# Stacked attentions of a four-layer transformer: masked keys placed by transfers through DRAM into tiles of kept zeros, and routing steps in other slots

## What is computed

```python
x = x + xattn0(layernorm(x), ctx); x = x + ffn0(layernorm(x))      # prototypes, low rank
x = x + xattn1(layernorm(x), ctx); x = x + ffn1(layernorm(x))      # shared and routed experts
x = x + xattn2(layernorm(x), ctx, mask); x = x + ffn2(layernorm(x))  # 8 experts, top 2, capacity
x = x + xattn3(layernorm(x), ctx)                                  # causal mask
h = layernorm(x, scale, shift); x = x + self_attention(h)          # causal, 128 keys
x = x + moe(layernorm(x, scale, shift))
# in ffn2: position of a token at its expert = running count over all tokens; beyond cap it is dropped
# every attention: softmax(q k^T / sqrt(8)) v, then Wo
```

## Time and profile before

| quantity | value |
|---|---|
| runs | 4140.27, 4146.7, 4158.86 us; median 4146.7 |
| the profiled execution, own time | 4131.0 us |
| its span | 4128.9 us |
| granted TensorE clock, mean | 0.909 |
| busy: PE, DVE, ACT, POOL | 3458.1, 3417.6, 2382.1, 1545.5 us |
| `a_km` products on GpSimd (L698) | 186, 631.3 us busy |
| `s_km` products on GpSimd (L698) | 62, 223.6 us busy |

### The profile page before, as it was taken

The page is one execution under the profiler, slowest core; times in us unless marked ns, Lnnn a source line. Parts: engine busy times, 40 slices in busy tenths (PEclk is TensorE's granted clock), DMA queues, the critical chain, the costliest instruction groups (busy, mean ns, idle before and its releaser), DMA issues. The chain is left out here.

```text
span 4128.9 us, 95016 instructions
## 1 busy us (share of the span) xinstructions
PE 3458.1 (84%) x31907; PEld 2505.8 (61%) x31907; DVE 3417.6 (83%) x6484; ACT 2382.1 (58%) x4440; POOL 1545.5 (37%) x935
## 2 busy tenths in 40 slices
PE   6983979998599788888568839989499998899999
PEld 3553647766477465565456627667366666677777
DVE  7888879999799788878755579889788888788888
ACT  2431657776277466655545527667576665466665
POOL 1210035553000345555444435545155563122222
PEclk9985989999599899989788969999699998899999
DMA  2001322222100222222121142222222222000000
GB/s 65 14 25 64 130 50 64 66 61 53 42 1 0 50 56 55 60 56 56 52 76 57 58 127 64 59 60 58 64 58 48 53 57 77 24 16 15 15 10 16
DMA packets 161066, 209.96 MB, mean 51 GB/s; under 512 B 38044, under 2 KB 110048, under 8 KB 157857
## 3 DMA queue, kind: packets, MB, share of 16 engines
q1 hardware_dynamic: 151457, 187.83, 16.8%
q0 software_dynamic: 8192, 16.92, 1.2%
q10 hardware_dynamic: 1152, 1.57, 0.2%
HBM read 53.09 MB, written 42.21 MB: 23 GB/s over the span
## 5 line engine op out<-in xcount | busy, mean ns | idle before, releaser
L1102 ACT ACTIVATE a_p<-a_p 128x480 f32<-128x480 f32 x832 | 501.7, 603 | 528.5 <-DVE a_p L939 521.8
L698 POOL TENSOR_TENSOR a_km<-a_k,a_slots 96x1920 fp32r<-96x1920 f32 x186 | 631.3, 3410 | 184.9 <-DMA a_k<-a_kh 181.2
L934 DVE TENSOR_REDUCE a_mx<-a_sc 128x4 f32<-128x480 f32 (+1 forms) x832 | 540.6, 650 | 129.8 <-PE a_sc L1206 106.4
L939 DVE TENSOR_TENSOR a_p<-a_sc,a_mx 128x480 f32<-128x480 f32 x832 | 531.8, 639 | 19.7 <-DVE a_mx L934 0.5
L1108 ACT ACTIVATE a_pt<-a_tp 120x512 f32<-120x512 f32 x832 | 485.4, 584 | 104.0 <-PE a_tp L1215 101.6
L1215 PE MATMUL a_tp<-ident,a_p 128*120 128x128 f32 x3328 | 518.9, 280 | 6.1 <-ACT a_pt L1108 6.1
L1200 PE MATMUL a_sc<-a_km,a_qr 96*128 96x480 f32 x768 | 403.5, 525 | 103.0 <-DVE a_p L939 71.5
L1215 PEld LDWEIGHTS a_tp<-ident,a_p 128*120 128x120 f32 x3328 | 414.7, 141 | 84.8 <-issue 37.2
L1239 PE MATMUL a_nd<-a_pt,a_vm 120*32 120x128 f32 x6656 | 297.6, 285 | 19.2 <-ACT a_pt L1108 18.8
L1200 PEld LDWEIGHTS a_sc<-a_km,a_qr 96*128 96x128 f32 x768 | 149.0, 194 | 210.4 <-issue 116.6
L2196 ACT ACTIVATE f_s<-f_pu 128x512 f32<-128x512 f32 x256 | 153.5, 600 | 212.4 <-PE f_pv L1678 212.4
(11 more groups left out here) (455 smaller groups left out, 8840.3 us busy)
## 6 DMA issues: line engine op xcount, KB each, us to landing
a_qr<-a_qh SPq DMA_DIRECT2D x372, 64.0 KB, 2.0
a_k<-a_kh SPq DMA_DIRECT2D x384, 60.0 KB, 2.0
a_ctx<-in_ctxT SPq DMA_DIRECT2D x64, 240.0 KB, 2.7
a_qr<-a_ql SPq DMA_DIRECT2D x186, 64.0 KB, 2.0
a_k<-a_kl SPq DMA_DIRECT2D x192, 60.0 KB, 2.0
dispatched<-f_empty SPq DMA_DIRECT2D x8, 1040.0 KB, 20.9
f_xr<-dispatched SPq DMA_DIRECT2D x32, 260.0 KB, 2.6
chosen<-f_none SPq DMA_DIRECT2D x8, 1024.0 KB, 11.8
```

The source lines that it names most:

```text
L698: v.tensor_tensor(KM[par][:, i, :, :].rearrange("p b (j k) -> p b j k", k=KN), K3[:, i, :, :].unsqueeze(2).to_broadcast([TR, GB, 4, KN]), ...
L934: v.tensor_reduce(mx[:], view, AX.X, ALU.max).then_inc(mx_ready, 1)
L939: v.tensor_tensor(PR[s % 4][:].rearrange("p (h k) -> p h k", k=k), view, mx[:].unsqueeze(2).to_broadcast([P, heads, k]), ALU.subtract).the ...
L1102: a.activation(PR[s % 4][:], PR[s % 4][:], ACT.Exp).then_inc(exp_ready, 1)
```

## The change

The 12 transfers into `K3` and the four products on GpSimd are replaced from group 1 on. SP writes the high and the low part of a group's keys to a DRAM tensor `stacked_keys` (two transfers), waits until both have landed (`keys_kept`), and reads them back in 12 transfers, one for each of three terms and four classes, each into the blocks of `KM` where row class and column class agree. The other blocks stay zero: those of `KM[0]` from group 0's products, those of `KM[1]` from one memset on GpSimd before group 1. TensorE waits for all 12 once, at a group's first slot. SP's loop over the groups is written out. In `Route` two Newton steps share a slot, and most steps move to later slots; the gate products no longer follow their turns in the next slot but take the bank a second time.

```diff
             for n in range(4):
-                yield
+                if n % 2 == 1:
+                    yield
                 dve.wait_ge(self.chain, done)
...
-            yield from self.at("dve", self.GROUPS * b + 3, 13)
+            yield from self.at("dve", self.GROUPS * b + 4, 4)
...
-            yield from self.at("dve", self.GROUPS * b + 4, 4)
+            yield from self.at("dve", self.GROUPS * b + 4, 9)
...
-            yield from self.at("dve", self.GROUPS * b + 4, 6)
+            yield from self.at("dve", self.GROUPS * b + 4, 10)
...
-                yield from self.at("dve", g + 4, 10 - 10 * (g % self.GROUPS))
+                yield from self.at("dve", g + 4, 14 - 14 * (g % self.GROUPS))
...
                 i = g % self.GROUPS
-                yield from self.at("act", self.GROUPS * b + 3, 7 + 2 * i)
+                yield from self.at("act", self.GROUPS * b + 3, 5 + 7 * i)
                 act.wait_ge(self.normed, b + 1)
...
                 last.then_inc(self.lh_ready, 1)
-                yield from self.at("act", self.GROUPS * b + 3, 9 + 2 * i)
+                yield from self.at("act", self.GROUPS * b + 3, 9 + 5 * i)
                 act.wait_ge(self.rt_done, g + 1)
...
                 a.activation(self.HS[:], self.bank[:], ACT.Copy).then_inc(self.hs_ready, 1)
-                yield
+                self.uses[1] += 1
+                yield from self.at("act", self.GROUPS * b + 3, 11 + 7 * i)
                 act.wait_ge(self.lg_done, g + 1)
...
                              ACT.Copy).then_inc(self.l_ready, 1)
-                self.uses[1] += 1
-            yield from self.at("act", self.GROUPS * b + 4, 2)
+                self.uses[5] += 1
+            yield from self.at("act", self.GROUPS * b + 4, 8)
             act.wait_ge(self.d_ready, b + 1)
...
             for g in range(self.GROUPS * b, self.GROUPS * (b + 1)):
-                yield from self.at("act", g + 4, 5 - 5 * (g % self.GROUPS))
+                yield from self.at("act", g + 4, 10 - 10 * (g % self.GROUPS))
                 if g > 1:
...
-                yield from self.at("pe", self.GROUPS * b + 3, 9 + 2 * i)
+                yield from self.at("pe", self.GROUPS * b + 3, 10 + 5 * i)
...
                 self.uses[0] += 1
-                yield
+                self.held = (self.hs_ready, g + 1)
+                yield from self.at("pe", self.GROUPS * b + 3, 12 + 7 * i)
                 pe.wait_ge(self.hs_ready, g + 1)
+                self.take_bank(pe)
+                self.after_main(pe)
                 if g == 0:
...
                 last.then_inc(self.lg_done, 1)
+                self.uses[4] += 1
                 self.held = (self.l_ready, g + 1)
-            yield from self.at("pe", self.GROUPS * b + 4, 5)
+            yield from self.at("pe", self.GROUPS * b + 4, 10)
             pe.wait_ge(self.ones_ready, 2 * b + 2)
...
-            yield from self.at("pool", g + 4, 12 - 12 * i)
+            yield from self.at("pool", g + 4, 14 - 12 * i)
...
+
+        def parts_free(eng, step, g):
+
+            if step == "k" and isinstance(g, int) and g == 1:
+                for i in range(4):
+                    eng.wait_ge(k3_in[i], 48)
+            elif step == "k":
+                at_least(eng, keys_kept, 32 * (g - 1))
+            else:
+                for i in range(4):
+                    at_least(eng, q3_in[i], 48 * g)
...
 
+                kept_keys = R.keys[0:2 * P * GB * KN].rearrange("(n q s) -> n q s", n=2, q=32)
+
                 def stack_terms(g, par):
...
                     sp.wait_ge(low_ready["k"], g + 1)
-                    for i in range(4):
-                        at_least(sp, km_ready[i], g)
-                        for term, part in enumerate((HIGH, LOW, HIGH)):
-                            sp.dma_start(K3[32 * term:32 * term + 32, i, :, :].rearrange("p b k -> p (b k)"),
-                                         part["k"][32 * i:32 * i + 32, :].bitcast(F32)).then_inc(k3_in[i], 16)
+                    for n, part in enumerate((HIGH, LOW)):
+                        sp.dma_start(kept_keys[n].rearrange("q (i f) -> i q f", i=4),
+                                     part["k"][:].bitcast(F32)).then_inc(keys_kept, 16)
+                    sp.wait_ge(keys_kept, 32 * g)
+                    if par == 1:
+                        sp.wait_ge(keys_empty, 1)
+                    at_least(sp, sc_ready, (g - 1) * S)
+                    for term, n in enumerate((0, 1, 0)):
+                        for j in range(4):
+                            row = 32 * term + 8 * j
+                            sp.dma_start(KM[par][row:row + 8, :, :, j * KN:(j + 1) * KN].bitcast(F32),
+                                         kept_keys[n, 8 * j:8 * j + 8, :].rearrange(
+                                             "r (s k) -> r s k", k=KN)).then_inc(keys_in, 16)
                     sp.wait_ge(low_ready["q"], g + 1)
...
-                    groups_loop(sp, lambda g, par, first, last: stack_first() if first else stack_terms(g, par), 3)
+                    groups_in_full(lambda g, par, first, last: stack_first() if first else stack_terms(g, par))
...
-
-                def pair(g):
-                    ctx_load(g + 2, 0)
-                    stack_terms(g + 1, 1)
-                    ctx_load(g + 3, 1)
-                    stack_terms(g + 2, 0)
-
-                pairs_loop(sp, NG - 2, pair)
-                stack_terms(NG - 1, 1)
+                for g in range(1, NG):
+                    if g + 1 < NG:
+                        ctx_load(g + 1, (g + 1) % 2)
+                    stack_terms(g, g % 2)
...
-                    for i in range(4):
-                        at_least(pool, (k3_in if step == "k" else q3_in)[i], 48 * g)
+                    parts_free(pool, step, g)
...
-                    masked_keys(pool, nc.gpsimd, g, par, (0,))
-                    scatter(g - 1, 4, 3)
+                    scatter(g - 1, 5, 6)
...
-                    masked_keys(pool, nc.gpsimd, g, par, (1,))
-                    scatter(g - 1, 11, 2)
-                    masked_keys(pool, nc.gpsimd, g, par, (2,))
-                    scatter(g - 1, 13, 2)
-                    masked_keys(pool, nc.gpsimd, g, par, (3,))
-                    scatter(g - 1, 15, 3)
+                    scatter(g - 1, 14, 6)
...
                 masked_keys(pool, nc.gpsimd, 0, 0, (0, 2))
+                nc.gpsimd.memset(KM[1][:].bitcast(F32), 0.0).then_inc(keys_empty, 1)
                 if route:
...
                     if packed and j == 0:
-                        pe.wait_ge(km_ready[i], g + 1)
+                        if isinstance(g, int) and g == 0:
+                            pe.wait_ge(km_ready[i], 1)
+                        elif i == 0:
+                            pe.wait_ge(keys_in, 192 * g)
                         pe.wait_ge(q3_in[i], 48 * (g + 1))
...
         R.dispatched = nc.dram_tensor("dispatched", [E2 * CAP + 2 * NB * P, ROW], F32).ap()
+        R.keys = nc.dram_tensor("stacked_keys", [2 * P * GB * P], F32).ap()
         R.chosen = nc.dram_tensor("chosen", [2 * NB * P + SPARE, D], F32).ap()
```

More of the change, by code:

```diff
@@ L297, in __init__ @@
         self.main_last = None
-        self.uses = [0, 0, 0, 0]
+        self.uses = [0] * 6
     def at(self, engine, group, slot):
@@ L671, in attention_phase @@
             q3_in = [sem(n_(f"q3_in{i}")) for i in range(4)]
+            keys_kept, keys_empty, keys_in = (sem(n_(s)) for s in ("keys_kept", "keys_empty", "keys_in"))
         sc_ready, mx_ready, sub_ready, exp_ready = (sem(n_(s)) for s in ("sc_ready", "mx_ready", "sub_ready", "exp_ready"))
@@ L1056, in high_part @@
                     act.wait_ge(ready[step], g + 1)
-                    for i in range(4):
-                        at_least(act, (k3_in if step == "k" else q3_in)[i], 48 * g)
+                    parts_free(act, step, g)
                     a.activation(HIGH[step][:], src, ACT.Copy).then_inc(high_ready[step], 1)
@@ L2357, in unit @@
             return n // HB // (NT // E) * HB + n % HB
-        assert route.uses[0] == route.uses[1] and route.uses[2] == route.uses[3], (route.uses, route.now)
+        assert all(route.uses[n] == route.uses[n + 1] for n in (0, 2, 4)), (route.uses, route.now)
         route.now = dict.fromkeys(route.now, 10 ** 6)
```

## The result

The changed kernel took 4302.3 us (median of 4 runs, 4298.27 to 4308.67) where the kernel before took 4144.15 on the same chip: ratio 1.0381, 95% interval 1.0357 to 1.0406. That is 158 us slower; the forecast was 43 faster, the range ended at 4180. The profiled execution has a span of 4296.5 us, 167.6 above the one before.

A forecast was written before the change was run, and what follows sets the result against it. Layer 2's routed pairs were taken to be bound by VectorE, held behind GpSimd's instructions and waiting on routing. -79 + 4 + 30 + 2 = -43 us on the median 4146.7 gave 4104; range 4045 to 4180.

The forecast's parts named there:

- Held VectorE instructions: Layer 2's attention: small VectorE instructions no longer stand behind GpSimd's products; 5.5 us a pair off VectorE's busy time.
- the lower bound of -35: Layer 2's attention: only the holding goes and nothing of the waits, a routed pair at 75.8 us.
- Routing in other slots: Layer 2's attention: waits for `rt_hl` and value projections go; VectorE's idle time in a routed pair from 12.2 to 4.5 us.
- -79: Layer 2's attention: a routed pair takes 68.4 us instead of 81.6, over six pairs.
- The keys' way: Low part to first scores by writes, reads and query transfers: 17.9 us; the self-attention has 15.5, net +30 us there.
- their size does not bind: The twelve key reads: 0.031 us a piece on eight engines, 0.5 us a read, against 0.6 to issue each.
- Layers 1 and 3 at 0: Attention of layers 1 and 3: 21.7 us from low part to next first scores covers 17.9, costing 0.
- The rival of slow reads: Key reads take 1.0 us each, 22.7 us to first scores; self-attention +102, layers 1 and 3 +45; 4221 us; chance 0.15.
- Top 2 behind the attention: Behind layer 2's attention: the last batch's top 2 now falls there, +4 us.
- The memset: Clearing `KM[1]` on GpSimd before group 1 in four attentions: +2 us in all.

The follow-up runs named there:

- e5_both: The changed kernel with key tiles laid out class by class and the DRAM copy laid out as 128 rows; 4085.1 us, 0.9917 of the kernel before.
- e1_slots: The kernel before with only routing steps and scatters in the new slots, keys the old way; 4129.9 us, 1.0015 of the kernel before.
- e2_keys: The kernel before with only the keys through DRAM, routing and scatters in the old slots; 4243.3 us, 1.0304 of the kernel before.
- e10_after_shift: The changed kernel with 128 instructions of already met waits on TensorE ahead of layer 3's attention; 4283.1 us, 1.0319 of the kernel before.
- e11_before_shift: The kernel before with 128 instructions of already met waits on TensorE ahead of layer 3's attention; 4131.7 us, ratio 0.9962.
- e4_long: The changed kernel with key tiles laid out class by class, so a read moves 4 long pieces a row instead of 16; 4193.9 us, ratio 1.0181.
- c2_both_again: Same code as e5_both, run again on another chip; 4150.8 us, 1.0024 of the kernel before.
- d3_both_third: Same code as e5_both, run a third time on another chip; 4082.8 us, 0.9893 of the kernel before.
- c3: e5_both's short key path with routing and scatters in the old slots, on one chip with c2_both_again; 4161.1 us, 1.0043 of the kernel before.
- e8_shift: e5_both with 256 already met waits (128 more TensorE instructions) ahead of layer 3's attention; 4115.5 us, 0.9939 of the kernel before.
- e9_shift_twice: e5_both with 128 instructions of met waits on TensorE ahead of layer 3's attention and 128 ahead of the self-attention; 4126.0 us, ratio 0.9946.

## Why the prediction was wrong, point by point

- *Held VectorE instructions:* right in kind. 28.7 us were forecast for the three lines; 33.2 became 3.6 + 2.8 + 1.1 = 7.5, that is 25.7. VectorE's whole busy time in a routed pair fell from 69.41 to 62.47, 6.9 where I had 5.5 (the lower bound of -35 goes with 5.8, a slip of 2 us in all). In the self-attention the four normalisations take 1.02 us instead of 1.93, as reckoned.
- *Routing in other slots, and -79:* the mechanism was right in kind, on a chip without pauses. There e5_both's pairs take 69.9 us (68.4 forecast) and layer 2 534 us, 78 below the 612, which were measured on another chip. In the changed kernel's own trace the pair is 81.9 us, and layer 2 gave 16: new pauses took what the held instructions gave back. No row of before showed them. The two waits of the earlier trace rows do hang on the slots: they shrink in e1_slots and, for `rt_hl`, stay in e2_keys. But the two parts are no sum. With the products in place the slots were worth nothing (e1_slots 1.0015), since VectorE became 5.5 us a pair busier by new holding. On one chip the pairs take 80 to 83 us with the new slots alone, 73 to 75 with the products gone alone and 69.9 with both (602, 563 and 534 us in layer 2): some 4 us a pair for the slots, and only once GpSimd is free, where I had 7.7 (idle time from 12.2 to 4.5).
- *The keys' way, the step that failed:* 17.9 us were forecast from low part to first scores in the self-attention, 23.8 measured in the group shown (24.4 as the median). Its terms: the writes 8.7 where I had 7.5, near enough; the reads' issue 8.5 where I had 7.2 (0.7 us each, not 0.6); the queries' first transfers, from issue to scores, 6.5 where I had 3.2. The error that counts is "their size does not bind". I took eight engines at 0.031 us a piece of 512 bytes, 0.5 us a read, so that the reads would be over as they were issued and the queries behind them would land in 2.0 us. A read takes some 0.9 us: in the group shown the first nine land from 3152.9 to 3160.2. The twelve were in at 3165.06 only, the queries with them, 4.6 us behind their issue. That the queries would be last was right, and that the reads are what holds them up is my reading: with the reads issued twice as fast (e5_both) the first scores came no sooner behind the first read. 8.3 us late with the clock lost behind it is 9 a group, +134 in all, where I had +30.
- *Layers 1 and 3 at 0:* wrong by the same step. 21.7 us did not cover 22.9: 28.6 us a group instead of 27.6, +14. Layer 3 lost 24, and 16 of them are of this kind (e10_after_shift 458, e11_before_shift 442, both without stops); the other 8 are more stops after jumps.
- *The rival of slow reads* had this size of read (1.0 us, first scores at 22.7), got a chance of 0.15 and came nearest, 4221. Its reason, the price of small pieces, is not what e4_long shows; and it still counted on -79 in layer 2. 4221 and the 63 us that layer 2 did not give are 4284.
- *Top 2 behind the attention:* +4 forecast, and the stretch behind layer 2 grew by 4.6. That agreement is luck: the same stretch, in three runs of one and the same code, is 7.2 us shorter (c2_both_again), 4.8 longer (e5_both) or 10.1 longer (d3_both_third) than before. The memset: +2 forecast; with the first reads the stretch ahead of layer 2's scores grew by 6.

What stays open: what the pauses in layer 2 are, why they stand beside scatters and nowhere else, and why two of the chips do not have them. Shown is that neither the short pieces, nor the place of layer 3's code, nor the new slots are needed for them (c3 has them with the old slots, with 648 us). Open too is what makes a read take 0.9 us.

## What to carry to other kernels

Before a transfer is put on a path, write down the outermost size of both of its sides and how many rows it fills, and price it by rows of the trace that have the same ones: two writes of 256 KB each had landed 2.7 or 8.7 us after the first was issued, by nothing but the order in which the copy in DRAM was laid out. Price a chain of transfers by what lands last, and count what stands ahead of a transfer as part of its own time to land. Where an instruction waits for two things, look at both landings: the row named the keys, and the queries came last. A step moved out of one wait can move into the shadow of another engine's instruction; look at its own duration in the new place. And compare only what ran on one chip: a pause that one chip has and another has not was worth more here (70 us) than most edits.

## What was not expected of the hardware

- Twelve reads into eight rows each move some 77 GB/s together with pieces of 512 bytes (0.51 MB in the 6.6 us behind the window's seven empty slices) and 94 with pieces of 2048 (e5_both's window, ahead of the queries' transfers), where two writes of 128 rows reach 328 (mean of the 1.6 us window). The Trainium skill (SBUF — State Buffer, "Door 1: The DMA port swizzle (why `[64,N]` ≈ `[32,N]`)") lets the rate hang on how many ports the rows of a transfer reach; no run here changes the rows alone.
- The issue of a read took 0.71 us where its source was described as one run of 32 rows against a destination of 8 by 4, and 0.34 us where both were 8 by 4.
- A loop of TensorE in layer 3 stops in six of seven rounds (4.3 to 5.3 us in e5_both, each with two 16 KB loads of code beside it) or in none, by 128 instructions that stand ahead of it; the loads in that stage go from 65 to 12 with them (e8_shift). The 256 waits themselves lengthen the stretch they stand in by some 10 us (67.8 to 77.2 ahead of the self-attention in e9_shift_twice).
- The same kernel takes 4085.1 us on one chip and 4150.8 on another; the kernel before, 4125.8 and 4144.5 on these two.
